# Ten adding transfers of POOL in place of sixteen DVE additions: the first norm's part of the residual in an AdaLN layer

## What is computed

```python
h = _layernorm(x) * (1 + ca) + sa
x = x + ga * attn(h)            # attn(h) = h + LN(msg)*g1 + b1 + LN(mlp)*g2 + b2
h = _layernorm(x) * (1 + cb) + sb
x = x + gb * ffn(h)             # eight experts, top-k by expert, one expert per token
```

## Time and profile before

| what | value |
|---|---|
| time, median of 3 runs | 280.67 us (277.25 to 280.97) |
| span of the profiled execution | 278.9 us |
| busy in it: PE, DVE, ACT, POOL | 187.5, 178.5, 123.8, 129.5 us |
| stretch 38 to 72 us: PE, DVE, ACT, POOL busy | 29.99, 31.66, 16.01, 11.47 us |

### The profile page before, as it was taken

The page is one execution under the profiler, slowest core; times in us unless marked ns, Lnnn a source line. Parts: engine busy times, 40 slices in busy tenths (PEclk is TensorE's granted clock), DMA queues, the critical chain, the costliest instruction groups (busy, mean ns, idle before and its releaser), DMA issues.

```text
span 278.9 us, 4426 instructions
## 1 busy us (share of the span) xinstructions
PE 187.5 (67%) x1151; PEld 145.3 (52%) x1151; DVE 178.5 (64%) x668; ACT 123.8 (44%) x394; POOL 129.5 (46%) x207
## 2 busy tenths in 40 slices
PE   0788989796997788486658989550024995865730
PEld 0545759575776658472524475450014975864620
DVE  2679979999977665989898789600001993532330
ACT  2159964474697765448767443110011441232210
POOL 8737303143555444515991002777750045555652
PEclk9999999999799979757675899976555997999975
DMA  5890000001000000000665000633430324433300
GB/s 157 240 328 30 2 1 0 2 0 39 2 0 1 2 1 0 0 2 25 202 182 158 0 2 5 185 98 109 122 106 19 111 72 145 138 117 99 117 34 28
DMA packets 22009, 20.09 MB, mean 72 GB/s; under 512 B 2464, under 2 KB 19360, under 8 KB 21984
## 3 DMA queue, kind: packets, MB, share of 16 engines
q1 hardware_dynamic: 18752, 14.03, 16.9%
q0 software_dynamic: 2240, 5.51, 6.4%
q10 hardware_dynamic: 992, 0.27, 0.8%
HBM read 13.51 MB, written 6.29 MB: 71 GB/s over the span
## 4 chain that ended last, share of the span: by engine, by line
DVE 36%; PE 29%; another core or an unknown queue 14%; POOL 9%; issue 6%; ACT 4%; POOLq 1%; DVEq 0%
PE pH L940 7%; PE pQ L949 6%; DVE x_sb L1133 6%; DVE scr L1274 5%; DVE bn L988 3%; POOL yr L277 3%; DVE t L1085 2%; POOL rs L277 2%; PE pQ L655 2%; DVE x_sb L1086 2%; DVE rows L996 2%; PE pQ L850 1%; DVE t L1084 1%; DVE mv L991 1%
## 5 line engine op out<-in xcount | busy, mean ns | idle before, releaser
L404 POOL DMA_INDIRECT out_dram<-rows,gidx x28 | 28.4, 1014 | 38.2 <-DVE rows L1422 32.6
L401 POOL DMA_INDIRECT rows<-table_dram,gidx x28 | 27.3, 973 | 32.7 <-DVE gidx L1366 24.5
L940 PE MATMUL pH<-x_sb,hid 128*128 (+1 forms) x140 | 25.2, 309 | 20.3 <-issue 19.8
L949 PE MATMUL pQ<-ew,u 128*128 (+1 forms) x140 | 24.7, 303 | 18.6 <-DVE dig L1446 8.8
L621 ACT ACTIVATE u<-pH 128x256 f32<-128x256 f32 x35 | 13.3, 385 | 45.4 <-PE pH L940 30.1
L940 PEld LDWEIGHTS pH<-x_sb,hid 128*128 128x128 f32 x140 | 21.0, 215 | 21.8 <-issue 21.7
L949 PEld LDWEIGHTS pQ<-ew,u 128*128 128x128 f32 x140 | 20.3, 208 | 21.4 <-issue 12.1
L1414 DVE SCALAR_TENSOR_TENSOR t<-pQ,wslot,scr 128x128 f32<-128x128 f32 x35 | 12.1, 347 | 28.0 <-PE pQ L949 18.8
L1398 DVE COPY inv<-pL 128x105 f32<-128x105 f32 x1 | 0.3, 270 | 33.2 <-remote 33.2
L351 POOL TENSOR_TENSOR scr<-feat,z 128x512 f32<-128x512 f32 x8 | 9.6, 1202 | 23.0 <-DVE z L1112 23.0
L762 PE MATMUL pH<-qT,mall 128*128 128x512 f32 x32 | 18.0, 694 | 0.0
(11 more groups left out here) (316 smaller groups left out, 527.6 us busy)
## 6 DMA issues: line engine op xcount, KB each, us to landing
hid<-in_L_ffn_W_dram SPq DMA_DIRECT2D x35, 128.0 KB
table_dram<-x_sb SPq DMA_DIRECT2D x9, 256.0 KB, 2.8
x_sb<-in_L_attn_x_dram SPq DMA_DIRECT2D x8, 256.0 KB, 6.9
table_dram<-rows SPq DMA_DIRECT2D x7, 256.0 KB, 2.3
ew<-in_L_ffn_W_dram SPq DMA_DIRECT2D x2, 512.0 KB, 7.5
w1d<-in_L_ffn_W_dram SPq DMA_DIRECT2D x1, 1024.0 KB, 9.9
rows<-table_dram,gidx POOLq DMA_INDIRECT x28
out_dram<-rows,gidx POOLq DMA_INDIRECT x28
```

Source lines behind the costliest of these rows:

```text
L401: gp.indirect_dma_start(row[:, t, :], None, table[:, :], bass.IndirectOffsetOnAxis(gidx[:, t:t + 1], 0)).then_inc(gathered[t], 16)
L404: gp.indirect_dma_start(out.rearrange("b l d -> (b l) d"), bass.IndirectOffsetOnAxis(gidx[:, t:t + 1], 0), row[:, t, D:2 * D], None).then_ ...
L940: mm = te.matmul(pH[i % 2][:, f * P:(f + 1) * P], wcur[:, i % RW, f * P:(f + 1) * P], xt[:, bass.ds(i - e, 1), :], start=True, stop=True)
L949: mm = te.matmul(pQ[i % 2][:, 0:D], eh[:, i % 2, f * P:(f + 1) * P], ew[:, bass.ds(e, 1), f * D:(f + 1) * D], start=(f == 0), stop=(f == 1))
```

## The change

DVE keeps one operation of each `v_acc`, the product, and writes it over `xn` in place. Since `p_gt` reads `xn`, the product now waits for `gt_done`. The rest is done by ten adding transfers (a DMA that reads its destination, adds the source and writes it back), which POOL issues:

- `row_residual(b)`, twice: POOL copies the row `rD` of batch b out to 16 tiles in `h2` (128 x 2048 elements, 1 MB in all), waits for that copy, and issues a transfer that adds `h2` to the batch's half of `x_sb`.
- `residual(g)`, eight times: POOL waits until the batch's row transfer has landed (`row_added`) and until DVE's product is there (`res_ready`), and issues a transfer that adds `xn` of the group (256 KB) to `x_sb`.

`v_x1(g)` waits for the landing of `residual(g)`. The products also stand in another order: group by group from 0, where before it was 5, 6, 0, 1, 2, 3, 4, 7.

```diff
+            def row_residual(b):
+                gp.wait_ge(S["rows_done"], 1)
+                gp.tensor_copy(h2[:, b * TB:(b + 1) * TB, :], rD[:, b, :].unsqueeze(1).to_broadcast([P, TB, D])).then_inc(S["rD_spread"], 1)
+                gp.wait_ge(S["rD_spread"], b + 1)
+                gp.wait_ge(S["xn1"], GB * (b + 1))
+                gp.dma_start(x_sb[:, b * TB:(b + 1) * TB, :], h2[:, b * TB:(b + 1) * TB, :], accum_op=ALU.add).then_inc(row_added[b], 16)
+
+            def residual(g):
+                gp.wait_ge(row_added[g // GB], 16)
+                gp.wait_ge(S["res_ready"], g + 1)
+                gp.dma_start(bgroup(x_sb, g), xn[:, g], accum_op=ALU.add).then_inc(pulled[g], 16)
+
+            row_residual(0)
+
...
             for s in range(G + 6):
                 if s < G:
                     qprime(s)
+                if s == 1:
+                    row_residual(1)
+                if s < 4:
+                    residual(2 * s)
+                    residual(2 * s + 1)
...
             def v_acc(g):
                 b = g // GB
                 dve.wait_ge(S["rows_done"], 1)
-                link(dve.tensor_tensor(t2[:, :, :], xn[:, g], row4(rA[:, b, :]), ALU.mult))
-                link(dve.tensor_tensor(t2[:, :, :], t2[:, :, :], row4(rD[:, b, :]), ALU.add))
-                link(dve.tensor_tensor(bgroup(x_sb, g), bgroup(x_sb, g), t2[:, :, :], ALU.add))
+                dve.wait_ge(S["gt_done"], g + 1)
+                dve.tensor_tensor(xn[:, g], xn[:, g], row4(rA[:, b, :]), ALU.mult).then_inc(S["res_ready"], 1)
...
             def v_x1(g):
                 dve.wait_ge(S["yr_done"], g + 1)
+                dve.wait_ge(pulled[g], 16)
```

More of the change, by code:

```diff
@@ L178, in build @@
             den_ready z_done qp_done tq qT_done y1_ready m1_ready relu0 y2_ready sq1 sq2 u1_done u2_done yr_done x1_done x1_half
-            stats3 rs3 nm_done xn3 xn3_last tx3 h2_done h2_last lg_ready
+            res_ready rD_spread stats3 rs3 nm_done xn3 xn3_last tx3 h2_done h2_last lg_ready
             lmax exp2 probs prt_ready counts totals keys low_ready klo_ready over_ready sover_ready thr_bits thr_ready rsum_ready base_ready
@@ L186, in build @@
         ld_x = [sem(f"ld_x{g}") for g in range(G)]
+        row_added = [sem(f"row_added{b}") for b in range(B)]
         w_loaded = [sem(f"w_loaded{k}") for k in range(RW)]
-        gathered = [sem(f"gathered{k}") for k in range(R)]
+        pulled = [sem(f"pulled{k}") for k in range(R)]
         scattered = sem("scattered")
@@ L400, in gather @@
             def gather(t):
-                gp.indirect_dma_start(row[:, t, :], None, table[:, :], bass.IndirectOffsetOnAxis(gidx[:, t:t + 1], 0)).then_inc(gathered[t], 16)
+                gp.indirect_dma_start(row[:, t, :], None, table[:, :], bass.IndirectOffsetOnAxis(gidx[:, t:t + 1], 0)).then_inc(pulled[t], 16)
             def scatter(t):
@@ L927, in p_xt @@
             def p_xt(t):
-                te.wait_ge(gathered[t], 16)
+                te.wait_ge(pulled[t], 32 if t < G else 16)
                 te.transpose((pT, pF)[t % 2][:, 0:P], row[:, t, 0:D], ident[:, :]).then_inc(S["xt_ready"], 1)
@@ L1104, in _ @@
                     v_kvt(0)
-                    v_acc(5)
+                    v_acc(0)
             def v_z(g):
@@ L1219, in _ @@
                     prep_scales()
-                    v_acc(0)
+                    v_acc(3)
                 if s == 2:
-                    v_acc(1)
+                    v_acc(4)
+                    v_acc(5)
                 if s == 3:
                     v_kvt(1)
-                    v_acc(3)
+                    v_acc(6)
+                    v_acc(7)
                 if s == 0:
-                    v_acc(6)
+                    v_acc(1)
+                    v_acc(2)
                 if 0 <= s - 5 < G - 2:
@@ L1235, in _ @@
                     v_u2(s - 3)
-                if 2 <= s <= 3:
-                    v_acc(2 * s - 2)
-                if s == 4:
-                    v_acc(G - 1)
             v_last()
```

## The result

| | before | after |
|---|---|---|
| time, median (20 runs each) | 279.45 us (277.25 to 280.97) | 281.06 us (279.22 to 284.71) |
| ratio | | 1.0078, 95% interval 1.0054 to 1.0101 |
| span of the profiled execution | 278.9 us | 281.5 us |
| busy: PE, DVE, ACT, POOL | 187.5, 178.5, 123.8, 129.5 us | 187.8, 168.8, 124.2, 141.2 us |
| rA's operation to `v_x1(0)`, start to start | 27.16 us | 29.36 us |

The kernel is slower by 1.6 us in medians; 287.1 was forecast. The ratio leaves out the one run, 284.71 us, that is over 1.5% above the kernel's fastest. Every run's time is some 1.8 us above its span: the execution profiled after took 283.35 us, 2.3 above its kernel's median, and the one before some 280.7 us, 1.2 above.

What follows compares the result with a forecast made beforehand. The prediction took the DVE-POOL ring behind step 4 as the bound, its start set by `v_x1(0)`. POOL's terms summed to 33.6 us, making `v_x1(0)` 7.0 later; less 0.6, span 285.3, plus 1.8: 287.1 us, range 277 to 298.

Steps and rivals of the forecast that it cites:

- the ring: `v_x1` and statistics on DVE, POOL's root, POOL's `yr`, next `v_x1`: bounds behind step 4, 7.84 us per round.
- C: One POOL copy of `rD` to 2048 elements per partition: 2.1 us, between 1.9 and 4.2, counted twice.
- I: What issuing one transfer costs POOL: 1.25 us, between 0.36 and 1.76, counted eight times.
- R: A 1 MB row transfer from end of issue to landing: 7.5 us, counted twice; plain copy 5.0 as lower bound.
- the "doubled" end: Row transfer landing if reading the destination as well makes the data take twice the time: 8.5 us.
- The turning point: Two copies, eight issues and two landings at 22.8 us: `v_x1(0)` 0.6 us later, time unchanged; predicted values add to 29.2.
- The bound of DVE's relief: PE's idle time, 38 to 72 us, lets `v_x1(0)` gain at most 4.0 us; with 0.6 behind it, 4.6.
- The addition doesn't ride along: Rival: the addition rides along with the copy, a row landing takes the plain 5.0 us, time 282.1 us; chance 0.22.
- a third: Rival: the addition runs at a third of the rate, a row landing takes 12.0 us, time 296.1 us; chance 0.19.
- The products were never late: Rival: DVE's products come after POOL asks for them, 1 or 2 us more, some 289 us; chance 0.05.
- POOL is "never late": Rival: cheap issues and 5.0 us landings leave PE as bound, up to 4.6 us less, 276.1 us; chance 0.12.
- "within 2%": Outcome class for the whole kernel's time, 275.1 to 286.3 us; chance 0.43.

Runs made afterwards that it cites:

- rowtwice: The changed kernel with each of the two row transfers issued twice, each with its own wait for the landing, so `rD` is added twice: median 296.83 us.
- none: The changed kernel without the ten transfers and the two copies; DVE still makes the products, nothing adds them to `x_sb`: median 274.46 us.
- plain: The changed kernel with each adding row transfer replaced by a plain 1 MB one from `x_sb` to `h2`, `rD` not added: median 278.02 us.
- norows: The changed kernel without the two copies and two row transfers; eight group transfers remain, `rD` is not added: median 274.81 us.
- twoops: The changed kernel without copies and row transfers, DVE adding `rD` in place in `xn`; POOL issues the eight group transfers: median 277.32 us.
- early: The changed kernel reordered: both copies and row transfers ahead of the first `qprime`, transfers of groups 4 to 7 behind `qprime(3)`; nothing left out: median 275.62 us.
- late: The changed kernel reordered: second copy and row transfer behind `yrs(0)`, transfers of groups 4 to 7 behind the scales of steps 5 and 6: median 280.38 us.
- copyx1: `early` with the second copy of `rD` repeated on POOL behind `yrs(0)`, beside `v_x1(0)`, values unchanged: median 274.47 us.
- issuex1: `early` with the issues of `residual(6)` and `residual(7)` moved behind `yrs(0)`, beside `v_x1(0)`: median 274.91 us.
- pairs: `early` with the eight 256 KB group transfers made into four of 512 KB: median 273.75 us.
- bcast: `pairs` without copies, the row transfers reading `rD` itself 16 times over in rows of 512 bytes: median 278.20 us.

## Why the prediction was right or wrong

**The mechanism was right.** POOL's line of two copies, eight issues, two landings, two `qprime` and `yrs` sets the start of `v_x1(0)`; the spacing of the ring stays at 7.85 us; behind it nothing moves but with it. `rowtwice` and `none` show the first from both sides.

**The terms C, I and R were too large**, R and I above all, and this is the step that failed:

| term | predicted | measured | of the sum |
|---|---|---|---|
| 2R, landings | 15.0 | 6.39 + 6.50 = 12.9 | -2.1 |
| 8I, issues | 10.0 | 7.40, and two gaps of 0.3 | -2.0 |
| 2C, copies | 4.2 | 1.89 + 1.83 = 3.7 | -0.5 |
| two `qprime` | 2.5 | 1.08 + 1.09 = 2.2 | -0.3 |
| `yrs` | 1.93 | 2.02 | +0.1 |
| sum | 33.6 | 28.8 | -4.8 |

R's lower end, 5.0 for a plain copy, came from a share of busy time of another queue and was 0.8 too high in itself (`plain`: 4.2); the "doubled" end, 8.5, grew from it. I was taken from the indirect gathers with their gap: a gather's 0.94 was near and the 0.30 behind it was not, since issues in a row come with none (0.88 to 0.90 each). C had the fill's rate as its lower bound, 1.9, and that is what it cost; halving `qprime` told nothing.

**The turning point held.** At 2C + 8I + 2R = 22.8 the start was to come 0.6 us later than before. Measured were 24.6 (28.8 less `yrs` and the two `qprime`), so 0.6 + 1.8 = 2.4 us later by that rule; it was 2.2, and the missing 0.2 is what `yrs` and the two `qprime` took less.

**The bound of DVE's relief** named the right engine, PE, but its 4.0 us agree with the measured 27.16 - 23.15 = 4.0 by luck. The idle time was taken from 38 to 72 us, and `v_x1(0)` starts at 64.08: up to 64 us PE had been idle 26.00 - 24.21 = 1.8 us only (`none`, above). Of the rest, 1.4 us are those for which `yr` had lain ready, and 0.8 in the squares' time aren't resolved by the busy times. In the change's own trace none of this can be seen, for POOL's line ended later than PE's.

**From the line to the time.** The forecast was 6.0 us too high. 4.8 are the sum above. Against it stand 0.3 + 0.7 = 1.0 us between the search and the end, of which the prediction had nothing. That makes 3.8 in the span (285.3 against 281.5). The 1.8 us added on top were right: every run's time is that much above its span, 283.35 against 281.5 here. The other 2.3 are scatter between executions. The one profiled of the change took 283.35 us where the median is 281.06. I had also built on 280.67 us, the median of three runs before; over 20 it is 279.45.

**DVE's busy time** fell by 9.7 us, not 13: the products took 9.84 us for 5.36, 4.5 more (another operation, `ksel`, took 0.9 less). Of these 4.5, 2.2 had been on record before: the three additions of `rD` that took 1.4 us began at 43.56, 51.72 and 58.02 us, each beside a `qprime` (43.07, 51.22 and 57.33 us; the first and the last stand in the earlier trace rows). I counted this excess as leaving with the additions, and it passed to the products (7.52 us in `none`). The other 2.3 came with the copies and issues. I had called the product's new wait free and it was; its new neighbour was not, and I had not priced what POOL's work does to DVE.

**The rivals.** The addition doesn't ride along: 6.4 against 4.2 us. The time that this rival gave, 282.1, came out nearly right by luck: its two landings were 2.9 us too short and the other terms 2.7 too long. With the prediction's fixed 1.5 us taken off, the data of the adding transfer took 4.9 us against the plain one's 2.7, an estimate of 1.8 times: near the doubled rate, far from a third. The products were never late in the change, where both waits at `residual` ended with a DMA; they were in `plain`, `norows` and `twoops`. POOL is "never late" in `early`, the case that turns the sign, though by order and not by cheap transfers. The range, 277 to 298, held the time; 0.43 had been given to "within 2%".

**A miss among the variants.** `late` looked as good as `early` by the sum of POOL's line alone. It gave the relief back at 2.4 + 1.3 + 1.3 us because its work on POOL lay beside `v_x1`.

## What to carry to other kernels

Here, moving adds from a full engine to adding transfers paid only where the issuing engine hardly waited in order for a landing. Put the transfers that others depend on out first and let them fly beside its ordinary work (`early`, 4.9 us better than the change with the same work). Take them as large as the data allows, because an issue cost the same 0.9 us for 256 KB and for 1 MB in rows of 2 to 8 KB, and 2.27 in rows of 512 bytes.

Before placing POOL work in a gap, look at what DVE does there. `v_x1`, an operation of DVE with two SBUF operands on the critical chain, lost 1.6 us to a POOL copy of 1.9, and 0.65 us to an issue. The product at 47.17 us, beside an issue, lost nothing.

## What the runs showed of the hardware that was not expected

- DVE and POOL: two products in place took 4.80 us beside a `qprime` and a copy, 0.69 each without these; `v_x1`'s first half 4.31, 3.56 and 3.26 in place of 1.92 (`late`, `copyx1`, `issuex1`). The 1.92 itself lies beside a `qprime`; from group 4 on, where none is left, the same half takes 1.14.
- The end of the program grows with the number of direct transfers that POOL has issued long before: 5.9 us from the last scatter's issue to the end with none, 6.3 with 6, 6.5 with 8, 6.6 to 6.7 with 10, 6.9 with 12, some 0.08 us for each. Two plain ones count as adding ones do (`plain`), and those of 512 KB as those of 256 (`pairs`). What it is that takes this time stays open.
- TensorE's clock near 100 us. Before, four matmuls of the MLP took 3.27 us where `plain` took 1.88. PE in order of time, before:

```profile
101.66 3.27 PE L762 MATMUL pH<-qT,mall 128*128 128x512 f32 x4
```

and busy time by stretch, before and then `plain`, columns as in the earlier trace rows:

```profile
101.60:104.90 3.30, 3.30 (x8) 1.51 (x7) 1.77 (x7) 2.35 (x12) 1.46 (x1) 0.57 0.01 2
```

```profile
101.60:104.90 3.30, 3.30 (x24) 2.58 (x23) 2.08 (x8) 3.15 (x14) 1.15 (x1) 1.00 0.00 0
```

A granted clock of 0.57 is mostly the lower of its two levels (1.2 and 2.4 GHz), 1.00 the higher. The change has another such stretch, ahead of `v_x1(0)`, behind 2.59 us in which PE waited for `qprime(1)`:

```profile
51.60:55.10 3.50, 3.50 (x8) 1.51 (x7) 2.11 (x3) 1.14 (x8) 3.20 (x5) 0.54 0.60 117
```

The four matmuls there took 3.50 us in place of 1.88. Since POOL's line ended later still, they cost the time nothing. In `plain` such a stretch, with a granted clock of 0.62 from 54.8 to 59.3 us, does lie ahead of the squares that set the start.

The sixth ring step is 8.36 us long before, in the change and in `pairs`, 6.67 in `none`, `rowtwice`, `norows`, `twoops`, `early`, `plain` and `bcast`, and 6.82 to 6.97 in `late`, `copyx1` and `issuex1`. PE had waited 1.13 us for DVE just ahead in before and in `plain` alike, so the wait alone doesn't decide it, and with one profile of each kernel it stays open whether it goes by kernel or by execution. It is 1.7 us that the comparison of single spans must allow for (`plain` against the change, say), and a reason to compare kernels here by "rA to x1".
